# A cross-attention and mixture-of-experts kernel: score stacks with their rows interleaved, two-term stores, another prologue order, and a copy moved from ACT to DVE

## What is computed

```python
q = _heads(layernorm(x) @ W_Q.T + b_Q); k = _heads(ctx @ W_K.T + b_K); v = _heads(ctx @ W_V.T + b_V)
probs = softmax(q @ k^T / 4);  x = x + (probs @ v) @ W_O.T + b_O
xf = layernorm(x)
shared = (silu(xf @ sw1) * (xf @ sw3)) @ sw2
s = sigmoid(xf @ router_w.T); top-2 of s + router_bias; gates = s_sel / sum(s_sel)
x = x + shared + sum_e gate_e * (gelu(xf @ ew1[e]) @ ew2[e])
```

## Time and profile before

| | us |
|---|---|
| median of three runs | 433.05 |
| the three runs | 433.05, 446.2, 429.18 |
| the profiled execution | 430.49 |
| its span in the profile | 428.6 |
| PE busy | 389.7 (91%) |
| DVE busy | 308.0 (72%) |
| ACT busy | 204.2 (48%) |
| POOL busy | 129.0 (30%) |

### The profile page before, as it was taken

One profiled execution on the slowest core, in us unless ns is written; L12 is line 12 of the kernel. 1 busy time (PEld: TensorE's weight loads), 2 busy tenths in 40 slices (PEclk: granted clock), 3 DMA queues, 4 the chain that ended last, 5 costly groups with the idle time before them and its releaser, 6 DMA issues.

```text
span 428.6 us, 7142 instructions
## 1 busy us (share of the span) xinstructions
PE 389.7 (91%) x2760; PEld 237.0 (55%) x2760; DVE 308.0 (72%) x459; ACT 204.2 (48%) x366; POOL 129.0 (30%) x164
## 2 busy tenths in 40 slices
PE   5835999799989898989999999999999979999996
PEld 1625557433333232323337335348999869899996
DVE  4895995866979697975985931606578976587885
ACT  3531222456878687976883895572122202221221
POOL 7383005000303223241333213200038726205720
PEclk9975999857999799995999997599999969999999
DMA  7789767900907145260801010001002313101401
GB/s 251 253 216 257 189 166 148 277 4 4 192 9 171 30 91 114 69 134 4 187 15 54 2 50 5 4 0 53 0 27 85 96 41 100 49 2 50 127 23 49
DMA packets 27202, 38.56 MB, mean 90 GB/s; under 512 B 5536, under 2 KB 17184, under 8 KB 26400
## 3 DMA queue, kind: packets, MB, share of 16 engines
q1 hardware_dynamic: 27168, 38.10, 34.5%
HBM read 27.15 MB, written 10.49 MB: 88 GB/s over the span
## 4 chain that ended last, share of the span: by engine, by line
PE 65%; DMA 12%; DVE 11%; SPq 5%; issue 3%; ACT 2%; POOL 1%; ACTq 0%
PE psum L1031 36%; DMA QS<-qs_d 11%; PE psum L1177 11%; PE psum L1101 10%; PE psum L1108 5%; DVE xn L807 2%; DVE negm L931 2%; SPq L468 1%; DVE x_sb L917 1%; DVE nt L803 1%; ACT PB L707 1%; SPq L452 1%; DMA x_sb<-in_x_dram 1%; SPq L506 1%; SPq L481 1%
## 5 line engine op out<-in xcount | busy, mean ns | idle before, releaser
L931 DVE TENSOR_REDUCE negm<-psum 128x1 f32<-128x1024 f32 x128 | 154.5, 1221 | 39.5 <-PE psum L1108 38.8
L707 ACT ACTIVATE PB<-psum 128x512 f32<-128x512 f32 x256 | 139.1, 598 | 55.0 <-PE psum L1101 47.9
L1108 PE MATMUL psum<-KS,QS 48*128 48x512 f32 x304 | 97.5, 478 | 9.4 <-DMA QS<-qs_d 6.1
L1101 PE MATMUL psum<-QS,KS 50*128 50x512 f32 x256 | 100.0, 504 | 0.3 <-ACT PB L707 0.3
L1177 PE MATMUL psum<-PB,VA 128*17 128x256 f32 x1024 | 89.0, 424 | 2.1 <-ACT TMP L741 2.1
L1101 PEld LDWEIGHTS psum<-QS,KS 50*128 50x128 f32 x256 | 41.6, 206 | 55.2 <-ACT PB L707 44.2
L722 ACT ACTIVATE PB<-psum 128x512 f32<-128x512 f32 x40 | 22.1, 596 | 102.4 <-PE psum L1031 102.3
L625 POOL TENSOR_SCALAR R<-RAW 128x512 fp32r<-128x512 f32 x32 | 22.1, 689 | 109.2 <-PE psum L1031 79.8
L1108 PEld LDWEIGHTS psum<-KS,QS 48*128 48x128 f32 x304 | 40.0, 198 | 19.8 <-DVE negm L931 8.9
L1031 PE MATMUL psum<-XT,R 128*128 128x512 f32 x192 | 47.0, 394 | 0.0
L1177 PEld LDWEIGHTS psum<-PB,VA 128*17 128x17 f32 x1024 | 17.8, 98 | 51.3 <-issue 41.9
(11 more groups left out here) (131 smaller groups left out, 373.3 us busy)
## 6 DMA issues: line engine op xcount, KB each, us to landing
RAW<-in_ew_dram SPq DMA_DIRECT2D x32, 256.0 KB, 2.7
KS<-ks_d SPq DMA_DIRECT2D x16, 384.0 KB, 6.3
QS<-qs_d SPq DMA_DIRECT2D x16, 384.0 KB, 8.9
ks_d<-SWH SPq DMA_DIRECT2D x16, 256.0 KB, 3.4
ks_d<-SWH SPq DMA_DIRECT2D x16, 128.0 KB, 3.1
qs_d<-SWH SPq DMA_DIRECT2D x8, 256.0 KB, 5.7
RAW<-in_sw_dram SPq DMA_DIRECT2D x6, 256.0 KB, 2.9
x_sb<-in_x_dram SPq DMA_DIRECT2D x2, 512.0 KB, 6.1
```

The source lines that it names most:

```text
L707: act.activation(PB[:, n % PR, i * N:(i + 1) * N], bank[t % 3], ACT.Exp, scale=DK ** -0.5).then_inc(exp_done, 1)
L931: dve.tensor_reduce(negm[:, g % 2, r // QT, r % QT:r % QT + 1], psum[:, k0:k0 + 2, :].rearrange("p a n -> p (a n)"), AX.X, ALU.max, negate ...
L1101: pe.matmul(bank[t % 3], KS[s][rows, j, kp * P:(kp + 1) * P], QS[s][rows, j, :], start=True, stop=True).then_inc(scores_done, 1)
L1108: return pe.matmul(ring_bank(("max", m), half), QS[s][rows, j, qt * P:(qt + 1) * P], KS[s][rows, j, :], start=True, stop=True)
```

## The change

- The rows of a stack are interleaved: dimension d has rows 4d, 4d+1, 4d+2 of each half, for the three terms. Rows 3 and 7 are the bias rows. All other rows are zero, and matmuls take all 64 rows of a half. `KS` is first filled with a column of zeros with ones in the bias rows (ACT), `QS` with zeros (DVE for the first, POOL for the other two).
- Only two terms are stored, with one DMA per job (L438). A stack is loaded by three DMAs of 32 rows for `KS` and six of 16 rows for `QS`, and from the fourth group on two small ones that write zeros over old bias rows: 9 or 11 in place of 4.
- Prologue: POOL no longer makes the context's lo terms; DVE does. For the K and Q jobs of the second batch ACT writes the full sum as well as the hi term, and POOL makes the lo term. Both T jobs of the second batch come before the first maxima, the first 12 maxima steps run one pair in place of two, each second maximum is followed by a job, B comes last, and the stacks of groups 1 and 2 are loaded before the stores of the second batch.
- `LEAD` is 22 in place of 24.
- DVE makes all eight copies of the accumulator.

```diff
-LEAD = 24
+LEAD = 22
 TERMS = 3
-KROWS = TERMS * DK
 HP = P // 2
+RSTEP = HP // DK
+BIAS_ROW = TERMS
+ZERO_ROW = BIAS_ROW + 2 * RSTEP
...
-    jobs = [("T", 0, 0, 0), ("T", 0, 1, 0), ("K", 0, 0, 0), ("K", 0, 0, 1), ("Q", 0, 0, 0),
-            ("K", 0, 1, 0), ("K", 0, 1, 1), ("Q", 0, 1, 0)] + [("V", 0, i, 0) for i in range(4)]
-    jobs += [("T", 1, 0, 0), ("T", 1, 1, 0)]
+    jobs = [("T", 0, 0, 0), ("T", 0, 1, 0)]
+    for m in range(2):
+        jobs += [("K", 0, m, 0), ("K", 0, m, 1), ("Q", 0, m, 0)]
+    jobs += [("V", 0, i, 0) for i in range(4)] + [("T", 1, 0, 0), ("T", 1, 1, 0)]
+    FIRST_KQ1 = len(jobs)
     for m in range(2):
         jobs += [("K", 1, m, 0), ("K", 1, m, 1), ("Q", 1, m, 0)]
-    jobs += [("B", 0, 0, 0)] + [("V", 1, i, 0) for i in range(4)]
+    jobs += [("V", 1, i, 0) for i in range(4)] + [("B", 0, 0, 0)]
     NJ = len(jobs)
...
-    steps = [("stats", 0), ("rstd", 0), ("split", 0), ("split", 1), ("norm1", 0), ("split", 2), ("split", 3)]
+    steps = [("stats", 0), ("rstd", 0), ("split", 0), ("norm1", 0), ("split", 1), ("split", 2), ("split", 3)]
     steps += [("job", 0), ("job", 1), ("job", 2), ("mid", 0), ("mid", 1), ("job", 3), ("mid", 2), ("job", 4)]
-    steps += [("mid", 3), ("split", 4), ("mid", 4), ("stats", 1), ("rstd", 1), ("job", 5), ("job", 6), ("mid", 5)]
-    steps += [("norm1", 1), ("job", 7), ("split", 5), ("mid", 6), ("split", 6), ("mid", 7), ("ones", 1)]
-    m = 0
-    for n in range(8, NJ):
+    steps += [("mid", 3), ("mid", 4), ("split", 4), ("stats", 1), ("rstd", 1), ("job", 5), ("mid", 5)]
+    steps += [("norm1", 1), ("job", 6), ("mid", 6), ("job", 7), ("mid", 7), ("split", 5), ("split", 6)]
+    for n in range(8, FIRST_KQ1):
         steps.append(("job", n))
-        if n == 13:
+        if n == 9:
+            steps += [("zero", 1), ("zero", 2)]
+    steps += [("keys", 1), ("keys", 2), ("mid", FIRST_KQ1 - 2), ("mid", FIRST_KQ1 - 1)]
+    n = FIRST_KQ1
+    for m in range(LEAD):
+        steps.append(("max", m))
+        if m % 2 and n < NJ:
+            steps.append(("job", n))
+            n += 1
+        if m == UG - 3:
             steps.append(("wo",))
-        for _ in range(min(2 if n >= 11 else 0, UG - m)):
-            steps.append(("max", m))
-            m += 1
-        if n > 8 and n != LAST_KQ + 1:
-            steps.append(("mid", n - 1))
-        if n == LAST_KQ:
-            steps += [("mid", n)] + [("max", i) for i in range(m, UG)] + [("negmax", 0)]
-            m = UG
-        if n > LAST_KQ:
-            steps.append(("max", m))
-            m += 1
-    steps += [("mid", NJ - 1), ("clear",), ("ones", 2)] + [("max", i) for i in range(m, LEAD)]
+        if m == UG + 1:
+            steps.append(("negmax", 0))
+    steps += [("job", i) for i in range(n, NJ)] + [("mid", NJ - 1), ("clear",)]
...
+        kq_sum = U
...
-        qs_d = nc.dram_tensor("qs_d", (B, 2, 2, 3, DK, GH, S), F32, kind="Internal").ap()
-        ks_d = nc.dram_tensor("ks_d", (B, 2, 2, 3, DK, GH, T), F32, kind="Internal").ap()
+        qs_d = nc.dram_tensor("qs_d", (B, 2, 2, DK, 2, GH, N), F32, kind="Internal").ap()
+        ks_d = nc.dram_tensor("ks_d", (B, 2, 2, 2, DK, 2, GH, N), F32, kind="Internal").ap()
...
                 sp.wait_ge(job_free[n % 4], n // 4 + 1)
-                src = raw(parts[c % PARTS_RING])
-                for l in range(2):
-                    half = src[l * HP:(l + 1) * HP]
-                    if kind == "K":
-                        dst = ks_d[b, m, l, :, :, :, tb * N:(tb + 1) * N].rearrange("p d j t -> (d j) p t")
-                        sp.dma_start(dst[:, 0, :], half[:, 0, :]).then_inc(kq_stored[c][l], 16)
-                        sp.dma_start(dst[:, 1:3, :], half).then_inc(kq_stored[c][l], 16)
-                    else:
-                        dst = qs_d[b, m, l].rearrange("p d j t -> (d j) p t")
-                        sp.dma_start(dst[:, 0:2, :], half).then_inc(kq_stored[c][l], 16)
-                        sp.dma_start(dst[:, 2, :], half[:, 0, :]).then_inc(kq_stored[c][l], 16)
+                if c >= PARTS_RING:
+                    sp.wait_ge(kq_lo, c - PARTS_RING + 1)
+                dst = ks_d[b, m, :, tb] if kind == "K" else qs_d[b, m]
+                sp.dma_start(dst.rearrange("c d l j t -> (d l j) c t"), raw(parts[c % PARTS_RING]))\
+                    .then_inc(kq_stored[c], 16)
 
             def load_stack(g):
                 b, hg, s = g // HG, g % HG, g % SLOTS
                 m, l = hg // 2, hg % 2
-                stored_k, stored_q = kq_stored[kq_count(b, m):][:2], kq_stored[kq_count(b, m) + 2]
                 if g < SLOTS:
-                    sp.wait_ge(ones, g + 1)
+                    sp.wait_ge(ks_init, g + 1)
+                    sp.wait_ge(qs_init[g], 1)
                 else:
                     sp.wait_ge(scores_done, tiles_upto(UG * (g - SLOTS + 1) - 1))
+                    for r in (BIAS_ROW, HP + BIAS_ROW):
+
+                        sp.dma_start(raw(QS[s][r:r + 2 * RSTEP - 1:RSTEP, :, :]), raw(KS[s][ZERO_ROW:ZERO_ROW + 2 * RSTEP - 1:RSTEP, :, :]))\
+                            .then_inc(stk_loaded[s], 16)
                 for tb in range(2):
-                    sp.wait_ge(stored_k[tb][l], 32)
-                    sp.dma_start(raw(KS[s][tb * HP:tb * HP + KROWS, :, :]),
-                                 ks_d[b, m, l, :, :, :, tb * N:(tb + 1) * N].rearrange("p d j t -> (p d) j t"))\
+                    sp.wait_ge(kq_stored[kq_of[("K", b, m, tb)]], 16)
+                for c, term in enumerate((0, 0, 1)):
+                    sp.dma_start(raw(KS[s][c::RSTEP, :, :]), ks_d[b, m, term, :, :, l].rearrange("a d j t -> (a d) j t"))\
                         .then_inc(stk_loaded[s], 16)
-                sp.wait_ge(stored_q[l], 32)
-                for tb in range(2):
-                    sp.dma_start(raw(QS[s][tb * HP:tb * HP + KROWS, :, :]),
-                                 qs_d[b, m, l].rearrange("p d j t -> (p d) j t")).then_inc(stk_loaded[s], 16)
+                sp.wait_ge(kq_stored[kq_of[("Q", b, m, 0)]], 16)
+                for c, term in enumerate((0, 1, 0)):
+                    for tb in range(2):
+                        sp.dma_start(raw(QS[s][tb * HP + c:(tb + 1) * HP:RSTEP, :, :]), qs_d[b, m, term, :, l])\
+                            .then_inc(stk_loaded[s], 16)
...
-                if c == 4:
+                if c == 5:
                     load_stack(1)
-                if c == 8:
-                    load_bias(0)
                     load_stack(2)
+            load_bias(0)
...
-                elif st[0] == "split" and splits[st[1]][0] == "c":
-
-                    _, b, tb = splits[st[1]]
-                    c0 = b * T + tb * N
-                    pool.wait_ge(split_hi, st[1] + 1)
-                    pool.tensor_tensor(ctx_hl[1][:, :, c0:c0 + N], craw[:, :, c0:c0 + N],
-                                       raw(ctx_hl[0][:, :, c0:c0 + N]), ALU.subtract).then_inc(ctx_lo, 1)
-                elif st[0] == "ones":
-                    bias_ones(st[1])
+                elif st[0] == "job" and jobs[st[1]][0] in "KQ" and kq_of[jobs[st[1]]] >= PARTS_RING:
+                    n, c = st[1], kq_of[jobs[st[1]]]
+                    pool.wait_ge(kq_full, c - PARTS_RING + 1)
+                    pool.wait_ge(job_free[n % 4], n // 4 + 1)
+                    pool.tensor_tensor(parts[c % PARTS_RING][:, 1, :], kq_sum[c % 2],
+                                       raw(parts[c % PARTS_RING][:, 0, :]), ALU.subtract).then_inc(kq_lo, 1)
+                elif st[0] == "zero":
+                    pool.memset(raw(QS[st[1]][:, :, :]), 0.0).then_inc(qs_init[st[1]], 1)
...
-                        for done in kq_stored[c - PARTS_RING]:
-                            act.wait_ge(done, 32)
-                    act.activation(parts[c % PARTS_RING][:, 0, :], bank[n % 4][:, :], ACT.Identity,
-                                   bias=kq_bias(kind, m)).then_inc(kq_hi, 1)
+                        act.wait_ge(kq_stored[c - PARTS_RING], 16)
+                        if c >= PARTS_RING + 2:
+                            act.wait_ge(kq_lo, c - PARTS_RING - 1)
+                        act.activation(kq_sum[c % 2], bank[n % 4][:, :], ACT.Identity,
+                                       bias=kq_bias(kind, m)).then_inc(kq_full, 1)
+                        act.activation(parts[c % PARTS_RING][:, 0, :], bank[n % 4][:, :], ACT.Identity,
+                                       bias=kq_bias(kind, m)).then_inc(job_free[n % 4], 1)
+                    else:
+                        act.activation(parts[c][:, 0, :], bank[n % 4][:, :], ACT.Identity,
+                                       bias=kq_bias(kind, m)).then_inc(kq_hi, 1)
...
+                act.activation(KS[s][:, :, :].rearrange("p j t -> p (j t)"), one_col[:, 0:1].broadcast_to([P, GH * N]),
+                               ACT.Copy).then_inc(ks_init, 1)
...
-                elif st[0] == "evac" and st[1] < DVE_ENDS:
-                    g = st[1]
```

(26 more changed lines are left out.)

47 lines of the change are left out of this document (30 added, 17 removed).

## The result

| | before | after |
|---|---|---|
| median, four executions each on one chip, us | 431.12 | 388.13 |
| lowest to highest, us | 424.5 to 446.2 | 387.0 to 391.38 |
| profiled execution, us | 430.49 | 388.42 |
| its span, us | 428.6 | 386.6 |
| its mean granted clock | 0.916 | 0.987 |

The ratio is 0.911, with a 95% interval of 0.898 to 0.923; it leaves out executions more than 1.5% above the fastest of their kernel, so it is not the quotient of the two medians. The prediction was 399 us, with a range of 388 to 411: the direction held, and the time lies 0.1 us above the lower end of the range. Profile against profile the sum gave 398.7 and the execution took 388.4, so 10.3 us more were gained than it has.

The account below looks back on a forecast made before the run. Bounds: PE's prologue waits for DVE, held by POOL, stack waits and lower-clock stretches. Gains 8.2 + 9.0 + 3.7 + 13.3, less 2.0 and 0.4, give 31.8 off 430.5: 399 us, range 388 to 411.

Parts of the forecast that it names:

- Up to the first reduce: Prologue: with DVE still held by POOL's fills, first reduce at 34.3 instead of 42.5 us, 8.2 us gained.
- First reduce to first unit: Rest of the prologue: 28.9 us instead of 37.9, first unit at 63.2, 9.0 us gained.
- First units: Units right after the prologue: a shorter stretch at the lower clock, 3.7 us gained.
- the clock falls once more, but for some 12 us: First units: about 12 us at the lower clock instead of 20.7, so 5.2 of 8.9 us are lost again.
- the clock holds: Rival for the first units: no clock fall there, 5 us less, 394 us; chance 0.25.
- Stack loads: Groups: a load of 9.7 us fits its room of 12.6, no waits; 13.3 us gained, 7.2 by the clock.
- The copy on DVE: Accumulator copies at group ends: PE waits about 0.7 us instead of 0.36, six times, 2.0 us lost.
- Two more units with maxima: Groups: two more units carry maxima, 0.4 us lost.
- 64 rows where 48 or 50 were: the matmuls have the same columns, no term: Matmuls over the stacks: using more rows was given no cost or gain.
- Behind unit 105 nothing changes: Late part of the kernel, after unit 105: no time gained or lost.
- The prologue gives half: Rival: DVE held as before, or first units wait for bias rows; 8.6 us less gain, 407 us; chance 0.15.
- the loads take the far end: Rival in the groups: stack waits of 2.6 us remain and the clock falls as before, 419 us; chance 0.09.

Follow-up runs that it names:

- early fills: The changed kernel with POOL's two fills of QS moved ahead, right behind the first batch's normalisation: 385.04 us, ratio 0.890.
- the experiment: The kernel before with LEAD 22 and score matmuls over 64 rows, the added rows zeros: 404.84 us, against 410.86 with 50 rows.

## Why the prediction was right or wrong

The prediction held in its direction and, barely, in its range. The low end of that range was meant for a held clock with fills that cost DVE nothing. The clock did hold in the first units of the profiled execution, but the fills cost 2.4 us, and 5 us that made up for it came from a stretch at which the prediction expected nothing. So that the time is inside the range is in part luck.

- **Up to the first reduce**: forecast 34.3 and 8.2 us gained, measured 34.9 and 7.7. Its mechanism was right, DVE held by POOL's fills, and two pieces were off in opposite directions. The fills cost DVE 2.4 us, not 3.6, and it was through its two lo terms at 27.65 where 28.9 was forecast. PE's last value jobs then took 5.46 us in place of 3.24, because they ran at the lower clock (0.50 in the window from 28 to 32 us; 3.13 at full clock with early fills). The row for this was there: before, the same 24 matmuls took 5.14, and the sum priced them by jobs at full clock.
- **First reduce to first unit**: forecast 28.9, measured 29.9. A row of four reduces takes 4.95 us with its wait, not the 4.58 that 2 x 2.29 gives, so the first twelve maxima are some 1.3 us longer. Of the 8.1 us gained some 3 are the lead: with `LEAD = 22` alone the stretch from the first maxima to the first unit was 35.5 us in place of 38.7. The rest is the order of the jobs, which no run tried by itself.
- **First units**: forecast 3.7 gained, measured 8.3. Here the step "the clock falls once more, but for some 12 us" failed. In the changed profile the clock stayed at 1.00. With early fills (64 to 71 us), with the copy on ACT (67 to 71), with 24 units of lead (68 to 76) and with 26 (67 to 78) it did fall, in the same few units. So both the forecast and its rival, "the clock holds", describe executions of nearly the same kernel, and a single trace can't say which one will be timed.
- **Stack loads**: forecast a load of 9.7 us, no wait and 13.3 us gained, measured 9.3 to 10.7, no wait, and 13.6 in the five groups. The 13.6 are net of the copy: with the copy on ACT the same five groups take 103.5 us, so lead and loads gave 15.9 there and the copy took 2.3 back. The mechanism held, the term was 2.6 us too small. The Trainium skill (DMA: Bandwidth & Descriptors, "Rules for kernel authors") tells authors to coalesce many small transfers and calls those under 64 KB mostly overhead; the nine DMAs of 128 and 256 KB are above that, and the trace shows them, with the two small ones, taking less time than four. What the text had not weighed is that the lead alone would have done the same (103.6 us with the old loads): the new form of the loads wasn't needed for it. Its room of 12.6 us also takes off 1.4 for a wait that the earlier trace rows have at 1.13; nothing hangs on that.
- **The copy on DVE**: the sign was right, the term mis-sized. 2.0 us were forecast, 3.7 measured, because the wait is not 0.7 us but 0.82 five times and 1.55 once. It comes six times, not eight. This lies within its upper bound of 4.1.
- **Two more units with maxima**: 0.4 forecast. The group in question, the one with the last maxima, is 2.0 us longer. Of this 0.8 are the lead: with `LEAD = 22` alone it takes 27.9 us where it took 27.1, and 27.8 in the changed kernel with the copy on ACT. The other 1.2 are the copy's longest wait, 1.55 in place of 0.35, already counted above. With 24 units of lead the whole changed kernel was 1.0 longer, not shorter.
- **"64 rows where 48 or 50 were: the matmuls have the same columns, no term"** and **"Behind unit 105 nothing changes"**: these two sentences failed, and they are one error. The rows cost no PE time, but the late stretch at the lower clock went with them, 6.0 us in the experiment; in the two profiles the part from the last turn to the last copy of the accumulator is 5.2 us shorter. With the 4.6 us of the first units this is 9.8 of the 10.3 us by which the forecast was too high.
- **The rivals.** "The prologue gives half" and "the loads take the far end" did not come. For "slower" the overlap of the small DMAs was the argument, and the timeline with 26 units of lead bears it out. (The page of the Trainium skill that it names, DMA: Bandwidth & Descriptors, has the 2 us a DMA from DMAs that GpSimd issues; here SP issues them.)

## What to carry to other kernels

Before summing up waits, take the clock out: from each execution's span and mean granted clock, with the cost of an us at the lower level taken from one repeated piece of work. Leave out what passes at the lower clock while the engine stands idle. The measure turned times from 424 to 442 us into a quantity that lies within 1.2% of its mean, and within 0.3% for the changed kernel and its versions, and it showed that more than half of this gain was clock. Where a prefetch is late, first try the lead, one constant, before the form of the transfer. An edit that looks free because it has the same number of instructions and columns can still move the clock, and a bundle of gains can hide a loss: here the copy's 3.7 us.
